# Twelve buffer fills moved from between scatters to the front of the kernel

## The reference

```python
x = x + 0.5 * ffn(layernorm(x))      # 8 experts, 128 -> 512 -> 128, one expert chosen by argmax
x = x + attention(layernorm(x))      # 16 heads of 8
x = x + 0.5 * ffn(layernorm(x))      # the same weights again
```

## Time and profile before

| | us |
|---|---|
| median of 3 runs | 999.62 |
| lowest and highest run | 999.19, 999.98 |
| span of the profiled execution | 996.9 |
| median less span | 2.7 |
| PE, DVE, ACT, POOL busy | 907.5, 832.2, 750.2, 219.1 |

### The profile page before, as it was taken

The page is one execution under the profiler, slowest core; times in us unless marked ns, Lnnn a source line. Parts: engine busy times, 40 slices in busy tenths (PEclk is TensorE's granted clock), DMA queues, the critical chain, the costliest instruction groups (busy, mean ns, idle before and its releaser), DMA issues. The chain is left out here.

```text
span 996.9 us, 18005 instructions
## 1 busy us (share of the span) xinstructions
PE 907.5 (91%) x5949; PEld 385.6 (39%) x6023; DVE 832.2 (83%) x1404; ACT 750.2 (75%) x1507; POOL 219.1 (22%) x317
## 2 busy tenths in 40 slices
PE   5799927899999999999999999999999999965996
PEld 4699923322222222222222222222222222434996
DVE  6776628989999999999999999999999998768664
ACT  4367706978888888888888888888888888754774
POOL 3168841831000000000000100000100000024775
PEclk9989957999999999999999999999999999996998
DMA  7632135752220213202022120220202000051311
GB/s 262 194 96 73 41 116 190 238 192 63 58 61 16 62 34 81 62 17 62 15 73 74 31 62 15 73 54 28 75 30 64 29 23 17 2 169 48 105 63 44
DMA packets 65443, 75.14 MB, mean 75 GB/s; under 512 B 12896, under 2 KB 43784, under 8 KB 65352
## 3 DMA queue, kind: packets, MB, share of 16 engines
q1 hardware_dynamic: 58776, 60.98, 20.6%
q0 software_dynamic: 5120, 12.59, 4.1%
q10 hardware_dynamic: 1456, 0.41, 0.2%
HBM read 40.47 MB, written 33.49 MB: 74 GB/s over the span
## 5 line engine op out<-in xcount | busy, mean ns | idle before, releaser
L1574 DVE TENSOR_REDUCE maxima<-ps_m 128x2 f32<-128x1024 f32 x512 | 602.8, 1221 | 53.8 <-PE ps_m L1335 52.8
L1544 ACT ACTIVATE probs<-ps_s 128x512 f32<-128x512 f32 x1024 | 555.9, 600 | 109.5 <-PE ps_s L1381 77.7
L1381 PE MATMUL ps_s<-q,k 74*128 74x512 bf16 (+1 forms) x950 | 294.5, 385 | 3.0 <-ACT probs L1544 0.9
L1392 PE MATMUL ps_o<-probs,vs 128*32 128x512 f32 x2048 | 272.7, 605 | 0.7 <-ACT probs L1544 0.7
L1381 PEld LDWEIGHTS ps_s<-q,k 74*128 74x128 bf16 (+1 forms) x1024 | 79.5, 97 | 303.4 <-ACT probs L1544 217.1
L1335 PE MATMUL ps_m<-k,q 64*128 64x512 bf16 x1024 | 159.9, 385 | 13.8 <-ACT probs L1544 7.9
L1265 POOL TENSOR_SCALAR split<-top 128x16 bf16<-128x16 f32 x32 | 8.1, 253 | 445.8 <-DVE top L1590 428.7
L1335 PEld LDWEIGHTS ps_m<-k,q 64*128 64x128 bf16 x1024 | 49.1, 93 | 102.7 <-issue 58.1
L693 PE MATMUL ps_y<-W,hT 128*128 x624 | 83.8, 278 | 0.0
L1392 PEld LDWEIGHTS ps_o<-probs,vs 128*32 128x32 f32 x2048 | 40.3, 108 | 109.3 <-issue 95.1
L693 PEld LDWEIGHTS ps_y<-W,hT 128*128 128x128 f32 x624 | 77.0, 194 | 0.6 <-issue 0.4
(11 more groups left out here) (215 smaller groups left out, 586.3 us busy)
## 6 DMA issues: line engine op xcount, KB each, us to landing
k_rows<-parts SPq DMA_DIRECT2D x24, 384.0 KB, 4.5
sums<-oT SPq DMA_DIRECT2D x30, 256.0 KB, 3.6
q<-q_parts SPq DMA_DIRECT2D x75, 96.0 KB
k<-k_rows SPq DMA_DIRECT2D x15, 288.0 KB
token_rows<-x SPq DMA_DIRECT2D x16, 256.0 KB, 4.1
token_rows<-v_and_ctx SPq DMA_DIRECT2D x16, 256.0 KB, 3.6
k<-k_rows SPq DMA_DIRECT2D x15, 256.0 KB
q_parts<-parts SPq DMA_DIRECT2D x8, 384.0 KB, 3.4
```

The source lines that it names most:

```text
L1381: nc.tensor.matmul(ps_s[n % 3][:, :], k2[buffer(g)][0:contracted, j, kt * P:(kt + 1) * P], q2[buffer(g)][0:contracted, j, u * HALF:(u + 1) ...
L1392: last = nc.tensor.matmul(ps_o[32 * j:32 * (j + 1), :], vs[buffer(g)][:, kt, j, :], probs[:, s % 2, j, :], start=(kt == 0), stop=(kt == KT ...
L1544: nc.scalar.activation(probs[:, s % 2, j, :], ps_s[n % 3][:, :], ACT.Exp, scale=SCALE).then_inc(exped, 1)
L1574: nc.vector.tensor_reduce(maxima[:, :, pr, qt, kh], ps_m[slot][:, :, :], AX.X, ALU.max).then_inc(unit_free[slot], 1)
```

## The change

The fills are no longer interleaved with the scatters. POOL issues all twelve in the front, one after another, behind its second quad of the norm and ahead of the wait for the stored rows and the routing. A wait on POOL's own last norm instruction is put ahead of them.

```diff
@@ Front.gpsimd
             last.then_inc(self.normed_pool, 1)
+        pool.wait_ge(self.normed_pool, len(self.BY_POOL))
+        for n in range(self.setup.FILLED):
+            self.setup.gpsimd_fill(pool, n)
         pool.wait_ge(self.route.stored, 2 * 16 * QUADS)
         pool.wait_ge(self.route.routed, Route.FOUND)
@@ Tiles.gpsimd
         for t in range(TILES):
             scatter(t)
-            if self.setup and t < self.setup.FILLED:
-                self.setup.gpsimd_fill(pool, t)
```

## The result

The changed kernel takes 989.0 us (median of 6 runs, 988.72 to 994.55) against 999.4 (median of 6 runs of before, 997.61 to 1003.28). The ratio is 0.9903, 95% interval 0.9882 to 0.9923: 1.0% faster. Forecast were 989.7 and 1.0%. No run here was disturbed; the ratios in this document are estimates with their interval and not the quotients of the two medians.

What follows compares the result with a forecast made beforehand. POOL's issuing of scatters with fills between them was taken to bound the stretch from 126.84 to 140.27. Span 996.9 - 9.95 + 0 = 986.95, plus 2.7 to the median, gave 989.7 us (1.0% faster), range 987.8 to 991.6.

Steps and rivals of the forecast that it cites:

- The 2.7 us between the median and the span: Whole kernel: the median time was set 2.7 us above the profiled span, turning 986.95 into 989.65.
- The fills between the scatters: First expert stage: without fills between scatters, the last scatter moves from 137.71 to 127.76, a gain of 9.95 us.
- two bounds: Last scatter of the first stage: 127.76 by the second stage's scatter spacing, 127.72 by its lag behind DVE's last item.
- The reload follows: Loads of x before the attention: they follow the last scatter by the same 2.56 us; everything behind shifts by 9.95 us.
- The fills in the front cost nothing: POOL's idle time before the first gather: the fills take 13.6 us, end at 35.7, leave 8.3 us; cost 0.
- Their new neighbours: DVE's routing beside the front fills: contention costs 0, with a range of 0 to 3 us.
- Rival A: Routing in the front: fills delay DVE's steps, first gather 1 to 3 us late, 990.7 to 992.7; chance 0.08.
- The clock: PE at the attention's start: starts cold again at the same cost, 1.9 us either way.
- rival B: Attention: PE's clock falls and returns elsewhere, 3.8 us either way beyond the 1.9, 985.9 to 993.5; chance 0.06.
- The prediction's own sign that the shift is wrong: Attention, from the loads to the second stage: its length changes by more than 2 us.
- C: Scatters: still spaced over 2 us by the landing of the scatter six back, nothing moves, 999.6; chance 0.02.
- D: Front: fills over 2.8 us each do not fit and delay the first gather, 1001.6 and up; chance 0.02.

Runs made afterwards that it cites:

- half: Changed kernel, but six fills in the front and six still behind the first six scatters; 995.64 us, ratio 0.9957 to the kernel before.
- slack: Changed kernel with SLACK 8 in place of 4, so the gathers may run further ahead; 989.6 us, ratio 0.9905 to the kernel before.
- behind: Changed kernel, but the twelve fills moved from the front to behind the last scatter; 999.37 us, ratio 0.9995 to the kernel before.
- twenty: Changed kernel with twenty fills in the front instead of twelve, eight written twice; 993.88 us, ratio 0.9933 to the kernel before.
- late: Changed kernel, but the twelve front fills wait until DVE has chosen all experts; 993.34 us, ratio 0.9925 to the kernel before.
- again: The changed kernel once more, no edit, with a second profile; 990.79 us, ratio 0.9904 to the kernel before.
- early: Changed kernel, but the twelve fills ahead of POOL's share of the norm, behind the masks; 991.75 us, ratio 0.9903 to the kernel before.

## Why the prediction was right, step by step

**The number.** The forecast is in effect the median before less 9.95 us. The 2.7 us between the median and the span is not what lies around the span: in every execution with both on record, of any kernel here, the time is 1.76 to 1.94 us above the span. So the profiled execution of before was some 0.9 us faster than the median. The medians moved by 10.4 us in the first set and 9.2 in the second, the means by 9.7 and 9.9. That the time was met within 0.7 us is partly luck, since runs of one kernel scatter by more.

**The fills between the scatters** (9.95 us by two bounds) measured 10.11 from scatter 0 to 31, and 9.4 and 9.9 us from the first gather to the last scatter in two profiles. `half` shows that the cost is one of POOL's issuing time, fill by fill. The second expert stage was a good control: its 40.15 us for 31 steps became 39.99 here. That nothing more was to be had once the scatters end with the items is shown by `slack`.

**The reload follows** held: 2.57 us from the last scatter to the loads, 2.56 before, and `behind` shows that the loads hang on the later of the two, fills and landing.

**The fills in the front cost nothing** held, with one size off: they take 12.0 us and not 13.6, since the 0.17 us of idle time that I added for each does not show between two memsets (they are 1.005 us apart from start to start). It made the estimate of their end 35.7, over L422's start at 35.55; in fact they end at 34.35, 1.1 us clear of it.

**Their new neighbours.** 0 was right for twelve fills at this place. The reason that the prediction put first was not sound: L863 unslowed beside the fills says nothing about the steps of the routing, because it is a tensor-tensor form, and no run here has such a form slowed by a fill. The view that the earlier trace rows are from also has a `tensor_scalar` beside the fills, which the prediction passed over:

```profile
L849 DVE TENSOR_SCALAR hT<-ps_hb,w1s 128x128 f32<-128x128 f32 x26 | 7.9, 346 | 0.5
```

It takes 347 ns after the fills, so it was not held either. It reads PSUM, where the steps that `twenty` and `late` show held read SBUF. POOL's 9% beside L102 was the wrong thing to scale as well, since it is DVE that loses. Rival A, at 1 to 3 us, was the right mechanism at the right price, 3.0 and 3.5 us in `twenty` and `late`; here it is 1.1 us away. The rule of the Trainium skill, which I gave 0.1 us, told the kinds of steps apart correctly where the rows that the prediction used could not.

**The clock.** The term was put at the same cost, 1.9 us either way. PE starts cold again, as forecast, but the clock is back within about 4 us of its restart and not 9 (0.87 in the window 136 to 138): the first pair of 512-column products (L1420) takes 1.13 us in the changed kernel, 2.07 before. From the loads to the first store of keys the changed kernel is 0.70 us shorter. `again` (1.12), `half`, `early` and `late` have that pair warm too, `twenty` (2.07) and `slack` (2.08) have it cold, so the moment of the return is not fixed by the change. The attention as a whole is 0.8 us longer in one profile and 3.5 in the other, by falls at 191 and at 868 of which each profile has only one. So rival B is partly true in each execution, over a larger part of the kernel than I looked at, and its bound of 3.8 us is about met; the median stayed in the range of 987.8 to 991.6. The prediction's own sign that the shift is wrong, over 2 us in the attention's length, came in `again` and not in the first profile: the shift as one block fits the mean times, not each execution.

**C and D** did not occur: the scatters are 1.29 us apart, and a fill takes 0.95 us beside a DMA share of 1.04 (22 to 36). One slip in the chances: the range reaches to 991.6 and so takes in 0.9 of the 2.0 us of A, a little under half and not over it.

## What to carry to other kernels

An engine that is busy for a fifth of the span can be the bound of one stretch: look for the place where all others wait, and count what the late engine issues there, item by item. If the same stage appears twice and only one of them carries the extra work, the other gives the price of taking it out. When work is moved into another engine's idle time, idle time is not the whole test: here twelve fills are free if they end before 35.4 and cost 3.5 us if they end at 41.7, though POOL idles through both, so check which forms of the neighbour's instructions they would stand beside.

## What the runs showed of the hardware

- A memset on POOL holds up a short `tensor_scalar` or cast of DVE on SBUF until it ends: 0.95 us for 0.18. Steps that read PSUM (L849, L229, L230) and steps of one element per partition (L235, L236) were not held. A row of such steps still advances: L430's 32 steps took 7.60 us beside 4.7 us of fills, 5.29 alone, with single steps of 0.24 to 1.03 us for 0.25, and the fills were not slowed (1.005 us apart in both).
- DVE's tensor-tensor and reduction forms took the same time beside the fills (L426 1.22 us, L419 0.42).
- A memset between two indirect DMAs costs POOL 0.84 to 0.88 us, less than its 0.95 us of busy time and less than the 1.005 us between two memsets.
- PE's granted clock fell at different places of the same program in two executions (191 to 198; 868 to 878), with 2.7 us of difference in the attention. That this is what scatters the times of one kernel by some us is likely, but only argued.
